# A wavelet convolution block: channel sums by row-wise matmuls, or by two rounded-part matmuls per tile with the means routed through DRAM

## The chip, the cores and the metric

One core of a Trainium2 chip runs the whole kernel. The metric is the device time of one execution in microseconds (us). The engines are TensorE (PE), VectorE (DVE), ScalarE (ACT), GpSimd (POOL) and SyncE (SP), whose queue issues most DMAs.

## The reference, cut to what matters

The input x is 8 images of 256 channels, 160x160 pixels. `haar_dwt` turns it into four bands of 80x80 pixels; a 1x1 convolution with batch norm and ReLU gives `fused` (256 channels). What the change touches is the spatial attention:

```python
avg_sp = jnp.mean(fused, axis=1, keepdims=True)
max_sp = jnp.max(fused, axis=1, keepdims=True)
sp_in = jnp.concatenate([avg_sp, max_sp], axis=1)
sp_map = conv7x7(sp_in)                       # one 80x80 map per image
spatial_out = jax.nn.sigmoid(sp_map) * fused  # the gate
```

Then come channel attention (mean and maximum of each channel of `spatial_out`, a small MLP, sigmoid), a 1x1 projection to 1024 channels with batch norm and ReLU, the inverse transform, and the addition of x.

## The kernel before, in words

**Tiles.** Each image is cut into 14 tiles of 6 or 5 rows of its 80x80 map (`ROWS`: 6, 6, 6, 6, 6, 5, 5, twice), so a tile has 480 or 400 pixels. Channels lie on the 128 partitions, in two halves. There are 112 tiles in all.

**Slots.** The program of every engine is a list of 133 slots. In slot k the first stage works on tile k (`fusion`, L497) and the last stage on tile k-21 (`project`, L483): the two run 21 tiles apart, since the attention of an image needs all of it. Slots 0 to 20 have a first stage only, slots 21 to 111 have both, slots 112 to 132 a last stage only. The engines meet by semaphores, and each works through its list strictly in order.

**First stage.** SP loads x. ACT rounds it to a high part (`x_hi`, L576), DVE takes the rest (`x_lo`, L746). PE multiplies in three products (high by high, high by low, low by high), 24 matmuls of 480 or 400 columns for each half of the input, so `fusion` is 48 matmuls. ACT writes the ReLU to `fused` (L658). `x_hi` of the next tile's first half can be written once `fusion` of this tile's first half is done, and its second half once the whole is.

**Last stage.** ACT and DVE split the gated tile into `y_hi` (L628) and `y_lo` (L824). PE projects, 48 matmuls, ACT and DVE form sums and differences (L606, L781, L783), DVE writes the pixels (`cells`, L801), and x is added, by an accumulating DMA from POOL's queue (L411), or in the last 21 tiles by DVE and POOL (L281). SP stores.

**Attention of image b-1**, in the first eight slots of image b (called phases 0 to 7):
- Channel sums: POOL adds the two halves of tile k-1 to `sm` (`channel_sum`, L404), after `x_lo` of the next tile's first half. PE sums over the partitions at the end of the slot (`add_channels`, L516): for each row one matmul of 80 columns, whose weight block `pick` has a single column of ones, so that the sum falls into that row's partition of `sums`. The operands are plain float32, and each such matmul shows as two records in the trace: 12 or 10 a slot.
- Channel maxima: DVE (L840, L849, L852), in phase 0 to DRAM and back into `maps[:, 1]` (SP, L351 and L362).
- Phase 1: ACT copies the means from `sums` into `maps[:, 0]` (L649), PE convolves after both halves of `fusion` (`convolve`, L525), ACT takes the sigmoid (L622), SP stores it to DRAM (L334).
- Phases 2 to 5: SP loads the sigmoid broadcast in chunks of 800 pixels (`sigb`, L328, the next one once the last was used), DVE gates two chunks a slot (`gate`, L817), ACT sums them in the next slot (`chunk_means`, L615).
- Phase 6: DVE reduces the partial results (`pool`, L886), PE starts the MLP (L563) at the slot's end. Phase 7: PE's `project` waits for the new channel weights and the first `y_lo`.

The orders of DVE, ACT, PE and SP within a slot stand in the four `body` functions. In the tail `cell` is a buffer of its own, and the last image's gate is loaded into the space of `xin` and `x_hi`.

Of the kernel before, what the change touches and what calls it, by code (L numbers as in the profile page):

```python
# [12 lines left out]
P = 128  # L13
# [31 lines left out]
def haar_block(nc, x, fusion_w, fusion_b, bn1_g, bn1_b, bn1_m, bn1_v, sa_w, ca_w1, ca_w2,  # L45
# [26 lines left out]
    map_dram = nc.dram_tensor("map_scratch", [1, NPX], F32, kind="Internal").ap()  # L72
    sig_dram = nc.dram_tensor("sig_scratch", [1, NPX], F32, kind="Internal").ap()
# [18 lines left out]
    with ExitStack() as ctx:  # L92
# [3 lines left out]
        def sem(name):  # L96
# [15 lines left out]
        cell = sb("cell", [P, XPM])  # L112
        sm = sb("sm", [P, PXM])
        sigb = sb("sigb", [P, CPX])
# [4 lines left out]
        pick = sb("pick", [P, 2 * GROUP - 1])  # L119
# [18 lines left out]

        mx = sd[:, 0, 0:PXM]
# [7 lines left out]


        last_gate = [xin[:, :, :].rearrange("p a b -> p (a b)")[:, 0:NPX // 2],
                     x_hi[:, :, :].rearrange("p a b -> p (a b)").bitcast(F32)[:, 0:NPX // 2]]  # L150
# [6 lines left out]
        tmp = cell[:, 0:4 * C].rearrange("p (q c) -> p q c", q=4)  # L157
# [8 lines left out]
        sums = pm[0:H2, 0:W2]  # L166
# [12 lines left out]
        ones_ready = sem("ones_ready")  # L179
        var_ready = sem("var_ready")  # L180
# [27 lines left out]
        sm_ready = sem("sm_ready")  # L208
        sum_psum = sem("sum_psum")
        across_psum = sem("across_psum")  # L210
        mean_ready = sem("mean_ready")
        maxima_ready = sem("maxima_ready")
# [28 lines left out]

        LL, LH, HL, HH = range(4)
# [43 lines left out]
        def _(sp):  # L286
# [43 lines left out]

            def store_sig(s):
                need(sp, mult_done, CT * NCH * s.nb)
                sp.wait_ge(sig_ready, s.nb + 1)
                sp.dma_start(sig_dram.rearrange("o (h w) -> (o h) w", w=W2), sig[:, :]).then_inc(sig_stored, 16)  # L334

            def body(s):
                if s.phase in GATED and s.a:
                    load_sig(s, GATED[s.phase][0])
# [44 lines left out]
        def _(gp):  # L383
# [3 lines left out]
            nc.gpsimd.memset(pick[:, :], 0.0).then_inc(pool_mem, 1)  # L387
            gp.wait_ge(pool_mem, 3)
            nc.gpsimd.memset(pick[:, GROUP - 1:GROUP], 1.0).then_inc(ones_ready, 1)
# [6 lines left out]
            def channel_sum(s):  # L396

                k = s.k - 1
                n = px_of(k)
                gp.wait_ge(f_ready, CT * (k + 1))  # L400
                if s.load_next:
                    gp.wait_ge(xlo_ready[0], s.k + 2)
                need(gp, sum_psum, k)
                nc.gpsimd.tensor_tensor(sm[:, 0:n], fused[:, 0, ring(k)], fused[:, 1, ring(k)],  # L404
                                        ALU.add).then_inc(sm_ready, 1)
# [34 lines left out]
        def _(pe):  # L440
# [29 lines left out]
            pe.wait_ge(ones_ready, 2)  # L470
# [35 lines left out]
            def add_channels(s):  # L506

                k = s.k - 1
                pe.wait_ge(sm_ready, k + 1)
                if s.phase == 1:  # L510
                    pe.wait_ge(mean_ready, s.nb + 1)
                for r in range(ROWS[k % TILES]):
                    row = FIRST[k % TILES] + r
                    at, base = row % GROUP, row - row % GROUP
                    m = min(GROUP, H2 - base)
                    mm = pe.matmul(sums[base:base + m, :], pick[:, GROUP - 1 - at:GROUP - 1 - at + m],  # L516
                                   sm[:, r * W2:(r + 1) * W2], start=(at == 0), stop=(at == m - 1))
                mm.then_inc(sum_psum, 1)

            def convolve(s):  # L520
                pe.wait_ge(mean_ready, s.nb + 1)
                pe.wait_ge(map_landed, 16 * (s.nb + 1))
                pe.wait_ge(band_pass, KS * NK)
                for j in range(NK):
                    mm = pe.matmul(conv, band[:, j, :], maps[:, j // KS, j % KS:j % KS + W2],  # L525
                                   start=(j == 0), stop=(j == NK - 1))
                mm.then_inc(conv_psum, 1)
# [44 lines left out]
        def _(act):  # L572
# [4 lines left out]

            act.wait_ge(var_ready, 2)
# [51 lines left out]

            def body(s):
                if s.phase == LAST:
                    act.wait_ge(hid_psum, s.nb + 1)
                    nc.scalar.activation(hid[:, :], squeezed, ACT.Relu).then_inc(hid_ready, 1)
# [11 lines left out]
                if s.phase == 1:  # L646
                    act.wait_ge(sum_psum, s.k - 1)
                    need(act, conv_psum, s.nb)
                    nc.scalar.activation(maps[:, 0, PAD:PAD + W2], sums, ACT.Copy, scale=1.0 / C  # L649
                                         ).then_inc(mean_ready, 1)  # L650
# [27 lines left out]
        def _(dve):  # L678
# [107 lines left out]
            def cells(s, i):  # L786
# [3 lines left out]
                if adding(s.kc, i):  # L790
                    need(dve, stored[g % 3], 16 * (g // 3))
                    to = xre[:, g % 3, 0:4 * n_px]
                else:
                    need(dve, added_v, plain_upto(g - 1))
                    need(dve, added_p, plain_upto(g - 1))
                    to = cell[:, 0:4 * n_px]
# [66 lines left out]

            def body(s):
# [18 lines left out]
                if s.phase == LAST - 1:  # L883
# [3 lines left out]
                    nc.vector.tensor_reduce(pool[:, :, 1], part[:, 1, :, :], AX.X, ALU.max).then_inc(pool_ready, 1)  # L887
                if s.phase in GATED:
# [56 lines left out]
```

## Time and profile before

| what | value |
|---|---|
| median of 3 runs | 2567.86 us (2566.55 to 2569.47) |
| profiled execution, its own time | 2566.07 us |
| its span, first to last instruction | 2564.3 us |
| PE matmul busy | 2429.5 us, 95% |
| DVE busy | 2066.0 us, 81% |
| ACT busy | 1072.1 us, 42% |
| POOL busy | 388.1 us, 15% |
| granted TensorE clock, mean | 0.987 |

The profiled execution lies 1.8 us below the median, and its span another 1.8 us below its own time. A row of a timeline gives start, length, engine, line, operation, output<-inputs and shape; in brackets stands the idle time of the engine before it and what ended that. "x12" is a merged row of twelve. Matmuls are pipelined, so the distance of their starts counts, not their length.

### The profile page before, as it was taken

Reading aid. Unit: us, or ns where it says so; the run is one execution under the profiler, and the core shown is the slowest. Engines: PE = TensorE matmul, PEld = TensorE weight load, DVE = VectorE, ACT = ScalarE, POOL = GpSimd, SP = SyncE. Lnnn points to the kernel's source line nnn. Section 1 sums busy time; section 2 is a strip of 40 time slices with the busy share of each in tenths; the row PEclk is TensorE's granted clock in tenths of the full one; section 3 lists DMA queues with packets and bytes.
Section 4 is the critical chain, followed back from the end, with each engine's and each line's share of the span. In section 5 each row is a group of like instructions: output and inputs, shape, how many; then the busy total and the mean of one; then the engine's idle time right before and its main releaser. Section 6 shows DMA issues by size and latency. Waiting matters only on the chain. (4 is left out here: it accounts for less than half of the span.)

```text
span 2564.3 us, 32151 instructions
## 1 busy us (share of the span) xinstructions
PE 2429.5 (95%) x12373; PEld 2121.6 (83%) x12373; DVE 2066.0 (81%) x2611; ACT 1072.1 (42%) x1421; POOL 388.1 (15%) x347
## 2 busy tenths in 40 slices
PE   5999999999999999999999999999999999986886
PEld 4888889898898978888898888989888888975765
DVE  4756778797778887788787987788877888779898
ACT  3444534354344533455334543445434453324222
POOL 0010111111111111111111111111111111122233
PEclk9999999999999999999999999999999999988999
DMA  4445699999999999999999999999999999886687
GB/s 142 159 159 178 183 279 273 269 294 262 253 276 272 294 254 258 281 273 285 261 265 271 287 271 271 270 274 292 256 260 268 281 291 258 232 286 243 247 289 281
DMA packets 110301, 660.26 MB, mean 257 GB/s; under 512 B 15362, under 2 KB 16452, under 8 KB 109892
## 3 DMA queue, kind: packets, MB, share of 16 engines
q1 hardware_dynamic: 83940, 487.80, 50.1%
q0 software_dynamic: 26208, 170.41, 36.5%
q8 instruction: 97, 1.59, 0.2%
q14 instruction: 56, 0.46, 0.0%
HBM read 448.04 MB, written 210.12 MB: 257 GB/s over the span
## 5 line engine op out<-in xcount | busy, mean ns | idle before, releaser
L483 PE MATMUL pp<-y_hi,wp_hi 128*128 128x480 f32 (+1 forms) x1792 | 677.4, 378 | 75.5 <-DVE y_lo L824 45.2
L746 DVE TENSOR_TENSOR x_lo<-xin,x_hi 128x1920 fp32r<-128x1920 f32 (+1 forms) x224 | 461.9, 2063 | 318.9 <-ACT x_hi L576 318.8
L576 ACT ACTIVATE x_hi<-xin 128x1920 fp32r<-128x1920 f32 (+1 forms) x224 | 418.1, 1867 | 671.1 <-PE pf L497 671.1
L497 PE MATMUL pf<-x_hi,wf_hi 128*128 128x480 f32 (+1 forms) x1792 | 677.7, 378 | 11.3 <-DVE wp_lo L741 6.2
L483 PE MATMUL pp<-y_lo,wp_hi 128*128 128x480 f32 (+1 forms) x1792 | 671.0, 374 | 0.0
L483 PE MATMUL pp<-y_hi,wp_lo 128*128 128x480 f32 (+1 forms) x1792 | 668.6, 373 | 0.0
L497 PE MATMUL pf<-x_hi,wf_lo 128*128 128x480 f32 (+1 forms) x1792 | 665.3, 371 | 0.0
L497 PE MATMUL pf<-x_lo,wf_hi 128*128 128x480 f32 (+1 forms) x1792 | 664.7, 371 | 0.0
L483 PEld LDWEIGHTS pp<-y_hi,wp_hi 128*128 128x128 f32 x1792 | 341.6, 191 | 133.9 <-DVE y_lo L824 61.1
L606 ACT ACTIVATE relu<-pp,t 128x480 f32<-128x480 f32 (+1 forms) x448 | 285.1, 640 | 397.3 <-PE pp L483 357.2
L801 DVE SCALAR_TENSOR_TENSOR xre<-sd,both 128x960 f32<-128x960 f32 (+1 forms) x364 | 410.3, 1169 | 6.5
L497 PEld LDWEIGHTS pf<-x_hi,wf_hi 128*128 128x128 f32 x1792 | 337.1, 188 | 62.4 <-DVE wp_lo L741 6.5
L483 PEld LDWEIGHTS pp<-y_hi,wp_lo 128*128 128x128 f32 x1792 | 341.4, 191 | 40.0
L483 PEld LDWEIGHTS pp<-y_lo,wp_hi 128*128 128x128 f32 x1792 | 341.2, 190 | 38.9
L411 POOL DMA_DIRECT2D xre<-in_x_dram x182 | 160.2, 880 | 1395.5 <-DVE xre L801 1395.5
L497 PEld LDWEIGHTS pf<-x_lo,wf_hi 128*128 128x128 f32 x1792 | 337.3, 188 | 40.0
L497 PEld LDWEIGHTS pf<-x_hi,wf_lo 128*128 128x128 f32 x1792 | 337.6, 188 | 37.0
L781 DVE SCALAR_TENSOR_TENSOR sd<-pp,nbias,relu 128x480 f32<-128x480 f32 (+1 forms) x448 | 308.1, 688 | 27.1 <-PE pp L483 16.5
L783 DVE SCALAR_TENSOR_TENSOR sd<-pp,nbias,relu 128x480 f32<-128x480 f32 (+1 forms) x448 | 306.4, 684 | 0.0
L658 ACT ACTIVATE fused<-pf,t 128x480 f32<-128x480 f32 (+1 forms) x224 | 138.6, 639 | 293.4 <-PE pf L497 275.0
L404 POOL TENSOR_TENSOR sm<-fused 128x480 f32<-128x480 f32 (+1 forms) x112 | 134.3, 1199 | 563.3 <-issue 293.7
L824 DVE SCALAR_TENSOR_TENSOR y_lo<-fused,ch,y_hi 128x480 fp32r<-128x480 f32 (+1 forms) x224 | 150.8, 715 | 1.0 <-ACT y_hi L628 1.0
(89 smaller groups left out, 1180.7 us busy)
## 6 DMA issues: line engine op xcount, KB each, us to landing
xin<-in_x_dram SPq DMA_DIRECT2D x160, 960.0 KB, 6.7
out_dram<-xre SPq DMA_DIRECT2D x160, 960.0 KB, 5.2
xre<-in_x_dram POOLq DMA_DIRECT2D x130, 960.0 KB, 9.3
xin<-in_x_dram SPq DMA_DIRECT2D x64, 800.0 KB, 6.5
out_dram<-xre SPq DMA_DIRECT2D x64, 800.0 KB, 4.5
xre<-in_x_dram POOLq DMA_DIRECT2D x52, 800.0 KB, 8.9
xre<-in_x_dram SPq DMA_DIRECT2D x30, 960.0 KB, 6.6
sigb<-sig_scratch SPq DMA_DIRECT2D x56, 400.0 KB, 7.9
```

The lines of the kernel that those rows point to most:

```text
L404: nc.gpsimd.tensor_tensor(sm[:, 0:n], fused[:, 0, ring(k)], fused[:, 1, ring(k)], ALU.add).then_inc(sm_ready, 1)
L411: nc.gpsimd.dma_start(xre[:, g % 3, 0:4 * px_of(kc)], dram(x_v, kc, i), accum_op=ALU.add).then_inc(x_added[g % 3], 16)
L483: mm = pe.matmul(pp[j][:, 0:n_px], w[:, kt, cols], y[:, s.pc, kt, 0:n_px], start=(kt == 0 and m == 0), stop=(kt == CT - 1 and m == 2))
L497: mm = pe.matmul(pf[o][:, 0:n_px].rearrange("p (y w) -> p y w", w=W2), w[:, i, q, o * P:(o + 1) * P], v[:, q % 2, :, q // 2, :], start=(i ...
L576: nc.scalar.activation(halves(x_hi, i, k), pairs(i, k), ACT.Copy).then_inc(xhi_ready[i], 1)
L606: nc.scalar.activation(relu[:, n, 0:n_px], pp[j][:, 0:n_px], ACT.Relu, bias=bias2[:, j * CT + i:j * CT + i + 1]).then_inc(r_ready, 1)
L658: nc.scalar.activation(fused[:, o, ring(s.k)], pf[o][:, 0:px_of(s.k)], ACT.Relu, bias=bias1[:, o:o + 1]).then_inc(f_ready, 1)
L746: nc.vector.tensor_tensor(halves(x_lo, i, k), pairs(i, k), halves(x_hi, i, k).bitcast(F32), ALU.subtract).then_inc(xlo_ready[i], 1)
L781: nc.vector.scalar_tensor_tensor(rows[:, :, 0, :], p, low, q, ALU.max, ALU.add).then_inc(sd_ready, 1)
L783: nc.vector.scalar_tensor_tensor(rows[:, :, 1, :], p, low, q, ALU.max, ALU.subtract).then_inc(sd_ready, 1)
L801: nc.vector.scalar_tensor_tensor(px[:, :, :, c], s0, both[:, c, i:i + 1], s1, ALU.add, op).then_inc(cell_ready, 1)
L824: nc.vector.scalar_tensor_tensor(y_lo[:, kc % 2, i, 0:n_px], fused[:, i, ring(kc)], ch[:, i:i + 1], y_hi[:, kc % 2, i, 0:n_px].bitcast(F32 ...
```

## The change

Five edits go together.

1. The sum over partitions is made for a whole tile at once. `sm` is split into `sm_hi` (ACT, rounded to float32r) and `sm_lo` (DVE, the rest), and two matmuls of 480 or 400 columns add the tile's sums into partition t of `sums`, t being the tile's number in the image. `pick` is float32r, with 14 of its columns used as weights.
2. ACT gets `sum_upper`, after `upper` and before `chunk_means` and the ReLUs of `fused`; DVE gets `sum_lower`, after `lower` and before the gate and `channel_max`. `add_channels` waits for `sm_lo`, POOL waits for `sm_lo` instead of the sum before it writes `sm` again.
3. The means now lie as 14 partitions of up to 6 rows, while the convolution wants one row in each of 80 partitions. ACT writes them to `means` (a part of `sigb`) at the head of phase 1; SP stores them to DRAM, waits, and loads them into `maps[:, 0]` with four DMAs (35, 5, 35 and 5 rows). `convolve` waits for these.
4. `cell` takes the space of `xin[:, 0]`, and the last image's gate that of `x_lo` and `x_hi`.
5. `pick` is built in `sm` and copied by ACT at the start.

```diff
+    mean_dram = nc.dram_tensor("mean_scratch", [TILES, PXM], F32, kind="Internal").ap()
-        cell = sb("cell", [P, XPM])
+        sm_hi = sb("sm_hi", [P, PXM], F32R)
+        sm_lo = sb("sm_lo", [P, PXM], F32R)
-        pick = sb("pick", [P, 2 * GROUP - 1])
+        pick = sb("pick", [P, 2 * TILES - 1], F32R)
+        means = sigb[0:TILES, 0:PXM]
+        cell = xin[:, 0, :]
-        sums = pm[0:H2, 0:W2]
+        sums = pm[0:TILES, 0:PXM]
+        ENDS = [t + 1 for t in range(TILES) if ROWS[t] < RMAX]
+        RUNS = list(zip([0] + ENDS[:-1], ENDS))
...
+            def store_means(s):
+                sp.wait_ge(mean_ready, s.nb + 1)
+                sp.dma_start(mean_dram, means).then_inc(mean_stored, 16)
+
+            def load_means(s):
+
+                sp.wait_ge(mean_stored, 16 * (s.nb + 1))
+                for t0, t1 in RUNS:
+                    rows = FIRST[t1 - 1] + ROWS[t1 - 1] - FIRST[t0]
+                    sp.dma_start(maps[FIRST[t0]:FIRST[t0] + rows, 0, PAD:PAD + W2],
+                                 mean_dram.rearrange("t (r w) -> (t r) w", w=W2)[t0 * RMAX:t0 * RMAX + rows, :]
+                                 ).then_inc(mean_landed, 16)
...
             def body(s):
+                if s.phase == 1:
+                    store_means(s)
+                    load_means(s)
                 if s.phase in GATED and s.a:
                     load_sig(s, GATED[s.phase][0])
...
-                need(gp, sum_psum, k)
+                need(gp, smlo_ready, k)
                 nc.gpsimd.tensor_tensor(sm[:, 0:n], fused[:, 0, ring(k)], fused[:, 1, ring(k)],
                                         ALU.add).then_inc(sm_ready, 1)
...
             def add_channels(s):
 
                 k = s.k - 1
-                pe.wait_ge(sm_ready, k + 1)
+                pe.wait_ge(smlo_ready, k + 1)
                 if s.phase == 1:
                     pe.wait_ge(mean_ready, s.nb + 1)
-                for r in range(ROWS[k % TILES]):
-                    row = FIRST[k % TILES] + r
-                    at, base = row % GROUP, row - row % GROUP
-                    m = min(GROUP, H2 - base)
-                    mm = pe.matmul(sums[base:base + m, :], pick[:, GROUP - 1 - at:GROUP - 1 - at + m],
-                                   sm[:, r * W2:(r + 1) * W2], start=(at == 0), stop=(at == m - 1))
+                t, n = k % TILES, px_of(k)
+                for part_of in (sm_hi, sm_lo):
+                    mm = pe.matmul(sums[:, 0:n], pick[:, TILES - 1 - t:2 * TILES - 1 - t], part_of[:, 0:n],
+                                   start=(t == 0 and part_of is sm_hi), stop=(t == TILES - 1 and part_of is sm_lo))
                 mm.then_inc(sum_psum, 1)
 
             def convolve(s):
-                pe.wait_ge(mean_ready, s.nb + 1)
+                pe.wait_ge(mean_landed, 16 * len(RUNS) * (s.nb + 1))
                 pe.wait_ge(map_landed, 16 * (s.nb + 1))
...
+            def mean(s):
+                act.wait_ge(sum_psum, s.k - 1)
+                need(act, mult_done, CT * NCH * s.nb)
+                nc.scalar.activation(means, sums, ACT.Copy, scale=1.0 / C).then_inc(mean_ready, 1)
+
+            def sum_upper(s):
+                n = px_of(s.k - 1)
+                act.wait_ge(sm_ready, s.k)
+                need(act, sum_psum, s.k - 1)
+                nc.scalar.activation(sm_hi[:, 0:n], sm[:, 0:n], ACT.Copy).then_inc(smhi_ready, 1)
+
             def body(s):
+                if s.phase == 1:
+                    mean(s)
...
-                if s.phase == 1:
-                    act.wait_ge(sum_psum, s.k - 1)
-                    need(act, conv_psum, s.nb)
-                    nc.scalar.activation(maps[:, 0, PAD:PAD + W2], sums, ACT.Copy, scale=1.0 / C
-                                         ).then_inc(mean_ready, 1)
+                if s.turn:
+                    sum_upper(s)
                 for c in GATED.get(s.phase - 1, ()) if s.phase else ():
                     chunk_means(s, c)
...
+            def sum_lower(s):
+                n = px_of(s.k - 1)
+                dve.wait_ge(smhi_ready, s.k)
+                need(dve, sum_psum, s.k - 1)
+                nc.vector.tensor_tensor(sm_lo[:, 0:n], sm[:, 0:n], sm_hi[:, 0:n].bitcast(F32),
+                                        ALU.subtract).then_inc(smlo_ready, 1)
...
+                if s.turn:
+                    sum_lower(s)
                 if s.phase in GATED:
                     gate(s, GATED[s.phase][0])
```

## Rows read from the trace of the kernel before

**Rows 1.** The page, its first part: busy us, share of the span, instructions
```profile
PE 2429.5 (95%) x12373; PEld 2121.6 (83%) x12373; DVE 2066.0 (81%) x2611; ACT 1072.1 (42%) x1421; POOL 388.1 (15%) x347
```

**Rows 2.** Timeline of PE, one full slot: one sum block to the next
```profile
1239.40 1.02 PE L516 MATMUL pm<-sm,pick 128*32 128x80 f32 x12
...
1240.67 0.38 PE L497 MATMUL pf<-x_hi,wf_lo 128*128 128x480 f32 x1
...
1261.23 0.38 PE L483 MATMUL pp<-y_lo,wp_hi 128*128 128x480 f32 x1
1261.54 1.02 PE L516 MATMUL pm<-sm,pick 128*32 128x80 f32 x12
```

**Rows 3.** Timelines of PE, ACT, DVE and POOL in the first image, one slot
```profile
155.16 1.02 PE L516 MATMUL pm<-sm,pick 128*32 128x80 f32 x12 [0.38 <-POOL sm L404]
...
161.73 1.94 ACT L576 ACTIVATE x_hi<-xin 128x1920 fp32r<-128x1920 f32 x1 [4.40 <-PE pf L497]
...
163.70 2.16 DVE L746 TENSOR_TENSOR x_lo<-xin,x_hi 128x1920 fp32r<-128x1920 f32 x1 [2.91 <-ACT x_hi L576]
...
165.99 1.21 POOL L404 TENSOR_TENSOR sm<-fused 128x480 f32<-128x480 f32 x1 [10.89 <-DVE x_lo L746]
...
166.26 1.32 ACT L658 ACTIVATE fused<-pf,t 128x480 f32<-128x480 f32 x2 [2.59 <-PE pf L497]
...
167.26 1.02 PE L516 MATMUL pm<-sm,pick 128*32 128x80 f32 x12 [0.38 <-POOL sm L404]
```

**Rows 4.** Waits between 60 and 226 us: total us, times, longest
```profile
PEld pm L516 <- POOL sm L404: 12.2, 14, 1.8
```

**Rows 5.** Groups by line and shape: busy us, mean ns, idle before
```profile
L658 ACT ACTIVATE fused<-pf,t 128x480 f32<-128x480 f32 x160 | 103.2, 660 | 240.2 <-PE pf L497 221.9 <-DVE y_lo L824 18.3
...
L840 DVE TENSOR_TENSOR sd<-fused 128x480 f32<-128x480 f32 x80 | 52.6, 658 | 67.3 <-ACT fused L658 67.1
```

**Rows 6.** Waits of DVE between 489 and 583 us: total us, times, longest
```profile
DVE x_lo L746 <- ACT x_hi L576: 7.8, 5, 4.7
DVE fused L817 <- DMA sigb<-sig_scratch: 2.7, 2, 2.4
```

**Rows 7.** Timelines of PE and DVE, end of the gated slots of that image
```profile
584.82 0.62 PE L516 MATMUL pm<-sm,pick 128*32 128x80 f32 x10
...
585.19 0.17 DVE L886 TENSOR_REDUCE pool<-part 128x2 f32<-128x16 f32 x1 [2.19 <-ACT relu L615]
...
599.92 0.48 PE L483 MATMUL pp<-y_hi,wp_hi 128*128 128x480 f32 x1 [2.67 <-DVE y_lo L824]
```

**Rows 8.** Timelines of SP and PE around the convolutions of images 0, 1 and 7
```profile
221.71 0.33 SPq L362 DMA_DIRECT2D maps<-map_scratch  x1
...
223.68 2.17 PE L525 MATMUL pm<-maps,band 80*80 80x80 f32 x28
...
458.04 0.32 SPq L351 DMA_DIRECT2D map_scratch<-maxima  x1
...
462.68 0.32 SPq L362 DMA_DIRECT2D maps<-map_scratch  x1
...
473.72 2.17 PE L525 MATMUL pm<-maps,band 80*80 80x80 f32 x28
...
2272.37 0.32 SPq L362 DMA_DIRECT2D maps<-map_scratch  x1
...
2277.22 3.99 PE L525 MATMUL pm<-maps,band 80*80 80x80 f32 x28 [4.68 <-issue]
```

**Rows 9.** Tile maps: DMA to landing of its 8 loads
```profile
DMA to landing us min/median/max: 1.6/3.3/8.1
```

**Rows 10.** Tile sig: DMA to landing of its 8 stores
```profile
DMA to landing us min/median/max: 4.5/6.3/8.5
```

**Rows 11.** Stretches: PE, PEld, DVE, ACT, POOL busy us, PEclk, DMA share, GB/s
```profile
595.00:607.00 12.00, 9.33 (x37) 7.63 (x35) 9.38 (x10) 6.44 (x10) 2.25 (x2) 0.86 0.77 224
...
2390.00:2540.00 150.00, 121.45 (x552) 100.40 (x550) 146.32 (x184) 42.50 (x69) 50.51 (x23) 1.00 0.82 291
```

More of the change, by code:

```diff
@@ L145, in haar_block @@
         junk = relu[:, :, :].rearrange("p a b -> p (a b)").bitcast(BF16)[:, 0:CPX]
-        last_gate = [xin[:, :, :].rearrange("p a b -> p (a b)")[:, 0:NPX // 2],
-                     x_hi[:, :, :].rearrange("p a b -> p (a b)").bitcast(F32)[:, 0:NPX // 2]]
+        cell = xin[:, 0, :]
+        last_gate = [v[:, :, :].rearrange("p a b -> p (a b)").bitcast(F32)[:, 0:NPX // 2] for v in (x_lo, x_hi)]
         stage = fused[:, 1, 2 * THIRD * W2:3 * THIRD * W2]
@@ L156, in haar_block @@
         pw = stage2[:, 0:NB * C].rearrange("p (t c) -> p t c", t=NB)
-        tmp = cell[:, 0:4 * C].rearrange("p (q c) -> p q c", q=4)
+        tmp = sd[:, :, :].rearrange("p a b -> p (a b)")[:, 0:4 * C].rearrange("p (q c) -> p q c", q=4)
         tmp2 = stage2[:, 8 * C:12 * C].rearrange("p (q c) -> p q c", q=4)
@@ L179, in haar_block @@
         ones_ready = sem("ones_ready")
+        pick_ready = sem("pick_ready")
         var_ready = sem("var_ready")
@@ L208, in haar_block @@
         sm_ready = sem("sm_ready")
+        smhi_ready = sem("smhi_ready")
+        smlo_ready = sem("smlo_ready")
         sum_psum = sem("sum_psum")
@@ L211, in haar_block @@
         mean_ready = sem("mean_ready")
+        mean_stored = sem("mean_stored")
+        mean_landed = sem("mean_landed")
         maxima_ready = sem("maxima_ready")
@@ L386, in _ @@
             nc.gpsimd.memset(maps[:, :, :], 0.0).then_inc(ones_ready, 1)
-            nc.gpsimd.memset(pick[:, :], 0.0).then_inc(pool_mem, 1)
+            nc.gpsimd.memset(sm[:, 0:2 * TILES - 1], 0.0).then_inc(pool_mem, 1)
             gp.wait_ge(pool_mem, 3)
-            nc.gpsimd.memset(pick[:, GROUP - 1:GROUP], 1.0).then_inc(ones_ready, 1)
+            nc.gpsimd.memset(sm[:, TILES - 1:TILES], 1.0).then_inc(ones_ready, 1)
             nc.gpsimd.affine_select(out=ident[:, :], in_=ident[:, :], compare_op=ALU.not_equal, fill=1.0,
@@ L469, in _ @@
             pe.wait_ge(wflo_ready, 4)
-            pe.wait_ge(ones_ready, 2)
+            pe.wait_ge(pick_ready, 1)
             def project(s, i):
@@ L576, in x_upper @@
                 nc.scalar.activation(halves(x_hi, i, k), pairs(i, k), ACT.Copy).then_inc(xhi_ready[i], 1)
+            act.wait_ge(ones_ready, 2)
+            nc.scalar.activation(pick[:, :], sm[:, 0:2 * TILES - 1], ACT.Copy).then_inc(pick_ready, 1)
             act.wait_ge(var_ready, 2)
@@ L795, in cells @@
                     need(dve, added_p, plain_upto(g - 1))
+                    dve.wait_ge(xlo_ready[CT - 1], NT)
                     to = cell[:, 0:4 * n_px]
```

## The prediction

> **What bounds the kernel now.** I read the page first: PE is busy 95% of the span, DVE 81%, ACT 42%, POOL 15% [rows 1]. An average over stages says little about one edit, so I cut the trace at PE's sum blocks, which close every slot. In slots 21 to 111, both stages at work, PE sets the pace. The reader should see in [rows 2] that a six-row slot takes 22.14 us from block to block, and that the 94 steps from the second `fusion` matmul (1240.67) to the last `project` matmul (1261.23) take 20.56 us, 0.219 us each. The 96 matmuls cost 21.0 us; the twelve small ones cost the other 1.14 us. Where PE alone is late, that is what the change can shorten.
>
> Three stretches obey something else. In the first image a slot takes 12.10 us (155.16 to 167.26) with 48 matmuls, 10.5 us: PE waits for POOL's `sm` in 14 slots [rows 3, 4]. There the sum block closes a loop: block, `fusion` of the first half, `x_hi` at 161.73, `x_lo` at 163.70, `sm` at 165.99 to 167.20, next block at 167.26. In the gated slots (phases 2 to 6) DVE is almost full: between 489 and 583 us it waits 7.8 us for `x_hi`, of which 4.7 ahead of the first gate, and 2.7 us for the gate's chunks, so some 6 us in four slots [rows 6]. In the last 21 slots DVE is busy 146.32 of 150 us [rows 11].
>
> **1. The sum block on PE.** Twelve small matmuls go, two of 480 columns come. None of 14 weight columns is in the trace; the nearest rows are those of 480 columns, 0.219 us a step, and these stream the same columns of the same type: 0.44 us. The other end: the old block needs 1.14 us for 12 x 80 = 960 columns, as many as two times 480; at its pace per column nothing is gained. I take 0.44. A six-row tile saves 0.70 us, a five-row tile (ten small matmuls, 0.95 us, against 0.36) about 0.6; 14 tiles save 9.6 us. I take 0.68 a block where PE is the bound.
>
> **2. `sum_upper` and `sum_lower`.** The nearest rows: ACT writes 480 columns in 0.66 us (L658), DVE combines two SBUF tiles of 480 in 0.66 (L840) [rows 5], some 0.6 when it streams behind another. In ordinary full slots ACT is idle when `sm` ends, and DVE waits for `fused` before `channel_max` (67.1 us over 80 tiles, 0.84 each, more than the 0.6 added) [rows 5]: cost nothing there.
>
> In the first image both lie on the loop. Behind `sm` now come 0.66 + 0.66 us and a second handoff, together 1.4 us, before the block starts; the block is 0.70 shorter. ACT also does `sum_upper` ahead of `fused` (which stood at 166.26), so `fused` comes about 1.7 us later, still in time for the shorter block's end. Slot: 12.10 + 1.4 - 0.70 = 12.8 us. For 19 slots, five-row ones a little less: **+13.5 us**. Slots 21 to 27 save 7 x 0.68: **-5 us**.
>
> **3. Full images with gated slots.** There are six such rounds of 14 slots (slots 28 to 111). Nine blocks of each are PE-bound: 9 x 0.68 = 6.1 us, one of them ahead of the first gate. In the other five slots (phases 2 to 6) DVE gets 0.6 us more each and PE asks for all 0.7 us sooner. I followed DVE from the first gate to `pool` at 585.19. Four `sum_lower` lie on the way, 2.4 us. Of the 6 us idle about 3.4 can be used up: the chunk wait shrinks only by the 0.6 of the one `sum_lower` between issue and use, and in two slots DVE still waits 0.5 us for ACT, which sums its chunks before it writes `fused`. So the chain gains 3.4 - 2.4 = 1.0 us where PE's blocks would give 3.4, and PE waits at the slot's end for `sum_lower` and `pool` (before: block at 584.82, `pool` at 585.19, met within 0.4 us [rows 7]). Phase 7 hangs on the same DVE chain (PE waits 2.67 us for `y_lo` at 599.92 [rows 7]) and moves with it. A round: 6.1 + 1.0 = 7.1 us; six: **-43 us**. Bounds: DVE gives back all (9.6 a round, -58), or the five slots gain nothing (-37).
>
> **4. The means through DRAM.** Before, ACT wrote them 5 us ahead of the convolution. Now: ACT writes 14 partitions of 480 at the head of phase 1 (0.66 us by L658; only `x_hi`, which waits for PE, is queued behind it), SP issues the store behind the load of the maxima (L362), waits S, issues four loads of some 0.3 us each, and the last lands after L. The route is 0.3 + S + 1.1 + L from L362's issue. L: 1.6/3.3/8.1 us [rows 9]. S: a small store took 4.5/6.3/8.5 [rows 10]; the maxima's took at most 4.6 (458.04 to 462.68) [rows 8]. I take 5.5. While SP waits, the load of tile k+2, the stores and residual loads stand behind it for some 5 us; the x load is for the tile after the next, most of a slot (22.14 us) ahead of its use, so nothing more is late.
>
> - Image 1 (images 2 to 6 alike): L362 at 462.68, convolution at 473.72, 11.0 us, 10.3 with the earlier block. Route 10.2: just in time. By the spread of L, two of the six meet a slow queue: about 4.5 us each, 9 us.
> - Image 0 has no last stage: 221.71 to 223.68 is 2.0 us. Route with a fast queue 0.3 + 4.5 + 1.1 + 1.6 = 7.5: 5.5 us late.
> - Image 7: 2272.37 to 2277.22 is 4.85 us, and the convolution waited for its map already. Route 10.8: 6 us late, and `project` of the next slot, the last gate's load and DVE behind them move along.
> - After a wait of 2.67 us for `y_lo` the granted clock averaged 0.86 over 12 us [rows 11]: part of it went at the lower level, 1.2 of 2.4 GHz, 1.7 us lost. I add it for two of the long waits, 3 us.
>
> Together **+23 us**. Lower bound: all hidden but images 0 and 7, +8. Upper: every image with the slowest store and load, 18 us against 10.3, 7.7 late each, about +60.
>
> A rule speaks for the lower bound: the Trainium skill, "DMA: Bandwidth & Descriptors", section "Anatomy of one DMA", gives a fixed cost of about 2.0 us for a DMA from GpSimd's queue. With S and L of 2 us, an estimate from that page, the route is 5.4 us, and only images 0 (3.4) and 7 (0.6) are late, +4 us. The trace's small transfers, behind 960 KB ones, took 3.3 and 6.3 in the median, so the sum goes by them.
>
> **5. The rest.** `cell`, the last gate's place and `pick` add one 14-to-27-column copy at the start: nothing. In the tail one block less of 0.7 us is hidden by DVE.
>
> **Sum.** 13.5 - 5 - 43 + 23 = -11.5 us. On the profiled execution 2566.07 becomes 2554.5 (span 2564.3 to 2552.8); on the median, 1.8 us above it, 2567.86 becomes **2556 us**.
>
> **The rivals.** What a measurement here can tell from no change is about 0.2%, 5.1 us.
>
> (a) *The route is hidden* in images 1 to 6: for it, half of the maxima's loads land within 3.3 us; against it, the slowest took 8.1. Part 4 is then +8, or +4 by the page's rule: 2537 to 2541. Chance 0.22.
>
> (b) *The convolution waits for the means in every image*: SP's store, wait and four loads take the place of ACT's copy. For it: the store lies on the queue behind a 960 KB store and beside POOL's accumulating load; against it: 10.3 us of slack. Price 7.7 + 1.7 us at the upper end for each of seven images and 6 to 10 for image 7, some +65: 2598 at most. It decides the sign from part 4 = 35 us, 4.4 us an image. With 6 us each, +50: 2583. Chance 0.14.
>
> (c) *TensorE's clock falls in the first image*, because PE now idles about 1.9 us of each 12.8. Price 1.7 us in up to 19 slots: +32, 2588. Against it: in the tail PE idled 19% of 150 us and the clock read 1.00 [rows 11]. Chance 0.04.
>
> (d) *The change doesn't do what it says*: float32r with 14 weight columns runs at the old pace. Then parts 1 and 3 vanish and `sum_lower` stays: 13.5 x 2 + 23 = +50 at the worst, 2618. Chance 0.04.
>
> My forecast itself, 2545 to 2565: chance 0.56.
>
> **How the numbers follow.** The range reaches down to (a) with a full gain in part 3 and up to the middle of (b): 2532 to 2580. Faster than 2562.7: all of (a) and four fifths of the forecast, 0.66. Within 0.2%: the forecast's edge and a little of (b), 0.16. Slower: (b), (c), (d), 0.18.
>
> **What would show it.** Right: the full slot measures about 21.4 us instead of 22.14; the first image's slot 12.8 instead of 12.10, with PE waiting for `sm_lo`; PE's block at the end of phase 6 waits for DVE; the waits list has the convolution waiting on DMA, long in images 0 and 7. Wrong: a two-matmul block of over 0.6 us, a PE clock under 1 in the first image, or a convolution that waits over 4 us in every image.

## The result, and the profile after

The changed kernel takes 2581.96 us (median of 6 runs, 2578.03 to 2586.69) beside 2568.66 us of the kernel before in the same comparison: ratio 1.0051, 95% interval 1.0036 to 1.0066. It is 0.5% slower where 0.5% faster was forecast, and lies just above the range. The profiled execution took 2583.17 us, its span grew from 2564.3 to 2581.4, by 17.1 us.

The page of the changed kernel, its first two parts (they answer to [rows 1]):

```profile
span 2581.4 us, 30569 instructions
...
PE 2386.6 (92%) x11317; PEld 2080.6 (81%) x11317; DVE 2127.0 (82%) x2723; ACT 1133.1 (44%) x1535; POOL 387.8 (15%) x347
...
PE   5888789999999999999999989999999999976886
...
PEclk9998899999999999999999999999999999988998
DMA  4444469999999989999999999999899999986687
```

PE has 43 us less to do and the kernel is longer all the same. The digits point at slices 2 to 6, the first image: PE reads 8, 8, 8, 7, 8 there, where every slice read 9 before, and its clock falls to 8 in slices 4 and 5.

The full slot, in PE's timeline of the changed kernel (it answers to [rows 2]), is as forecast:

```profile
1266.82 0.38 PE L545 MATMUL pm<-sm_hi,pick 128*14 128x480 f32 x1
1267.03 0.38 PE L545 MATMUL pm<-sm_lo,pick 128*14 128x480 f32 x1
...
1288.25 0.38 PE L545 MATMUL pm<-sm_hi,pick 128*14 128x480 f32 x1
```

21.43 us from block to block instead of 22.14. So part 1 holds: 0.7 us a block (a five-row slot falls from 18.65 to 17.96 us). Cutting both traces at the sum blocks, as the prediction did, gives the account in us (span after less span before):

| stretch | forecast | measured |
|---|---|---|
| start to slot 20, image 0's convolution (slot 15) left out | +13.5 | +42.8 |
| slot 15 | +5.5 | +4.0 |
| slots 21 to 27 | -5 | -3.0 |
| six rounds, slots 28 to 111 | -43, +9 for the means | -30.3 |
| slot 112 and the tail | +6 | +3.6 |
| clock after long waits | +3 | in the rows above |
| sum | -11 | +17.1 |

The prediction rounded part 4 down by half a microsecond, and so wrote -11.5. Of the 42.8 us in the first row, 1.5 come before the first block, 18.2 in slots 2 to 14 and 23.1 in slots 16 to 20.

**The first image.** The timeline of the changed kernel there (it answers to [rows 3]; in between, two slots):

```profile
151.46 0.38 PE L528 MATMUL pf<-x_lo,wf_hi 128*128 128x480 f32 x1
154.28 0.58 PE L545 MATMUL pm<-sm_hi,pick 128*14 128x480 f32 x1 [2.45 <-DVE sm_lo L910]
154.66 0.60 PE L545 MATMUL pm<-sm_lo,pick 128*14 128x480 f32 x1
155.06 0.60 PE L528 MATMUL pf<-x_hi,wf_hi 128*128 128x480 f32 x1
155.46 0.60 PE L528 MATMUL pf<-x_hi,wf_lo 128*128 128x480 f32 x1
...
168.49 0.39 PE L545 MATMUL pm<-sm_hi,pick 128*14 128x480 f32 x1 [1.70 <-DVE sm_lo L910]
...
178.70 1.21 POOL L435 TENSOR_TENSOR sm<-fused 128x480 f32<-128x480 f32 x1 [11.60 <-DVE x_lo L787]
179.94 0.60 ACT L671 ACTIVATE sm_hi<-sm 128x480 fp32r<-128x480 f32 x1 [3.57 <-POOL sm L435]
...
180.58 0.66 DVE L910 TENSOR_TENSOR sm_lo<-sm,sm_hi 128x480 fp32r<-128x480 f32 x1 [2.01 <-ACT sm_hi L671]
181.29 0.39 PE L545 MATMUL pm<-sm_hi,pick 128*14 128x480 f32 x1 [1.70 <-DVE sm_lo L910]
```

This slot, 168.49 to 181.29, follows no fall of the clock and takes 12.80 us, the forecast to the digit. But at 154.28, after 2.45 us of idling, PE goes on with matmuls 0.40 us apart instead of 0.22: the lower of the two clock levels, 1.2 GHz. The stretches of slots 2 to 14 (after and before; columns as in [rows 11]) show the sum of it: the clock averages 0.95 where it was 1.00.

```profile
62.30:232.00 169.70, 145.01 (x653) 123.99 (x654) 105.32 (x176) 68.41 (x66) 14.98 (x13) 0.95 0.43 143
```

```profile
60.80:212.30 151.50, 144.87 (x777) 125.62 (x777) 98.25 (x163) 63.36 (x53) 15.05 (x13) 1.00 0.48 161
```

**Slots 16 to 20** grew most, from 58.3 to 81.4 us. From the timelines of POOL, ACT and PE of the changed kernel, end of slot 18:

```profile
291.23 1.22 POOL L435 TENSOR_TENSOR sm<-fused 128x480 f32<-128x480 f32 x1 [15.86 <-DVE x_lo L787]
292.48 0.60 ACT L671 ACTIVATE sm_hi<-sm 128x480 fp32r<-128x480 f32 x1 [3.24 <-POOL sm L435]
292.99 0.85 ACT L646 ACTIVATE relu<-fused 128x800 bf16<-128x800 f32 x1
...
296.01 0.87 ACT L646 ACTIVATE relu<-fused 128x800 bf16<-128x800 f32 x1
...
296.88 1.19 ACT L699 ACTIVATE fused<-pf,t 128x480 f32<-128x480 f32 x2
297.67 0.67 PE L528 MATMUL pf<-x_hi,wf_hi 128*128 128x400 f32 x1 [3.23 <-ACT fused L699]
```

ACT works strictly in order, and `sum_upper` stands ahead of `chunk_means`. So ACT stood idle for 3.24 us until POOL's `sm`, then summed four chunks, and only then wrote `fused`, for which PE waited 3.23 us before the `fusion` of slot 19 (at 297.67). In the kernel before, the chunk sums came first and ended about when `sm` was ready, and `fused` followed at once:

```profile
260.41 1.22 POOL L404 TENSOR_TENSOR sm<-fused 128x480 f32<-128x480 f32 x1 [10.47 <-DVE x_lo L746]
...
262.01 0.19 ACT L615 ACTIVATION_READ_ACCUMULATOR relu<-fused 128x1 f32 x1
262.10 1.20 ACT L658 ACTIVATE fused<-pf,t 128x480 f32<-128x480 f32 x2
```

**The convolution** (it answers to [rows 8]). Waits over the whole span of the changed kernel (total us, times, longest), then its SP and PE around the convolution of image 7:

```profile
PE pm L545 <- DVE sm_lo L910: 52.9, 25, 6.3
...
PE pm L554 <- DMA maps<-mean_scratch: 15.1, 4, 8.4
DVE fused L859 <- DMA sigb<-sig_scratch: 14.3, 19, 1.5
```

```profile
2285.61 0.43 SPq L348 DMA_DIRECT2D mean_scratch<-sigb  x1
2291.97 1.29 SPq L355 DMA_DIRECT2D maps<-mean_scratch  x4
...
2294.38 4.03 PE L554 MATMUL pm<-maps,band 80*80 80x80 f32 x28 [8.43 <-DMA maps<-mean_scratch]
```

PE waited for the means in images 0, 2, 5 and 7: 2.89, 0.75, 3.00 and 8.43 us (the last against 4.68 before). The store of the means, from its issue to the issue of the loads, took 1.60 us in image 0, where no last stage moves data, 6.36 us here, and 7.23 us at most (image 5).

**The gated slots.** Slots 30 to 33 keep 0.7 us each in the six full images. Slot 34 (phase 6) gives it back: 21.35 us in the mean where it was 18.65. Its end on DVE and PE, second of the six images:

```profile
922.48 0.17 DVE L935 TENSOR_REDUCE pool<-part 128x2 f32<-128x16 f32 x1 [2.18 <-ACT relu L646]
...
922.64 0.57 DVE L910 TENSOR_TENSOR sm_lo<-sm,sm_hi 128x400 fp32r<-128x400 f32 x1
923.26 0.35 PE L545 MATMUL pm<-sm_hi,pick 128*14 128x400 f32 x1 [2.48 <-DVE sm_lo L910]
```

PE waits there for `sm_lo`, which stands behind `pool` in DVE's list, 2.3 us in the mean; in the kernel before, its block waited for nobody in these slots. This is the wait that the prediction named for the end of phase 6.

### The profile page after: what moved, and what is told of

It is laid out like the page before. It is cut to its first block and busy times, and to the rows that moved or that the text cites. A ratio compares the mean times of both kernels' runs of the same rounds, so it can differ in the third digit from the quotient of the medians.

```text
span 2581.4 us, 30569 instructions
## 1 busy us (share of the span) xinstructions
PE 2386.6 (92%) x11317; PEld 2080.6 (81%) x11317; DVE 2127.0 (82%) x2723; ACT 1133.1 (44%) x1535; POOL 387.8 (15%) x347
## 5 line engine op out<-in xcount | busy, mean ns | idle before, releaser
L528 PE MATMUL pf<-x_hi,wf_lo 128*128 128x480 f32 (+1 forms) x1792 | 672.3, 375 | 0.0
L528 PE MATMUL pf<-x_lo,wf_hi 128*128 128x480 f32 (+1 forms) x1792 | 671.5, 375 | 0.0
L528 PEld LDWEIGHTS pf<-x_hi,wf_hi 128*128 128x128 f32 x1792 | 342.8, 191 | 75.1 <-issue 19.4
L528 PEld LDWEIGHTS pf<-x_hi,wf_lo 128*128 128x128 f32 x1792 | 342.8, 191 | 40.4
```

Source lines behind the costliest of these rows:

```text
L528: mm = pe.matmul(pf[o][:, 0:n_px].rearrange("p (y w) -> p y w", w=W2), w[:, i, q, o * P:(o + 1) * P], v[:, q % 2, :, q // 2, :], start=(i ...
```

## The experiments

All but three edit the changed kernel; the ratio is to the kernel before, run on the same chip. Theory A at the start: ACT's order and the loop in the first image (with the clock that it lets fall), the route of the means, and something in the gated slots each take their part. Each was tested alone. The medians are of the execution times, while stretches are cut from the one profiled execution of each kernel.

### ACT's order

```diff
-                if s.turn:
+                if s.turn and s.c:
                     sum_upper(s)
                 for c in GATED.get(s.phase - 1, ()) if s.phase else ():
                     chunk_means(s, c)
+                if s.turn and not s.c:
+                    sum_upper(s)
```

> Edit: in the slots without a last stage (1 to 20), ACT sums the gated chunks (chunk_means) before it rounds sm (sum_upper), instead of after. Output as before. Theory A (the rounding, waiting for POOL's sm, holds back four chunk sums and with them fused and the next fusion): slots 17 to 20, 67.0 us together in the changed kernel against 46.2 before, fall to about 52; the gaps of 3.6 us between the two-matmul block and fusion vanish, and the whole becomes 12 to 16 us shorter, about 2567. Rival B (these slots are long because DVE waits for sm_hi ahead of its gate, whatever ACT's order): they stay within 3 us of 67.

2564.47 us (10 runs, 2558.21 to 2591.06), ratio 0.9989 (0.9962 to 1.0016). The same five slots in this kernel and in the changed one, by stretches:

```profile
249.20:313.10 63.90, 53.37 (x253) 46.09 (x253) 43.70 (x62) 38.91 (x57) 5.87 (x5) 0.98 0.59 188
```

```profile
249.50:330.90 81.40, 59.02 (x253) 50.38 (x253) 44.08 (x62) 39.43 (x57) 5.86 (x5) 0.88 0.47 154
```

17.5 of the 23.1 us are gone, and the clock is back from 0.88 to 0.98: the order of two calls on ACT cost about as much as all that slots 2 to 14 lost (18.2 us). The medians say 0.6%, some 16 us. The profiled execution is only 10.1 us shorter than the changed kernel's, since its six rounds took 8.4 us longer, for a reason that wasn't looked for.

### No route

The convolution waits for ACT's means in place of the loads; store and loads are gone, so the map of means that it reads stays zero.

```diff
-                if s.phase == 1:
-                    store_means(s)
-                    load_means(s)
...
-                pe.wait_ge(mean_landed, 16 * len(RUNS) * (s.nb + 1))
+                pe.wait_ge(mean_ready, s.nb + 1)
```

> Edit: the store and the four loads of the means are left out, the convolution waits for ACT's means only, and reads zeros in place of the means (left out: the mean's part of the map). Theory A (the route costs only where the convolution waits for its landing: about 4 us in image 0, 1 in image 2, 5 in image 5, 4 in image 7): 12 to 16 us shorter than the changed kernel. Rival B (SP held up by its wait delays loads and stores elsewhere, and costs more than the visible waits): over 25 us shorter. Rival C (the visible waits are covered by other waits): under 5 us shorter.

2569.66 us (2565.79 to 2577.36), ratio 0.9992 (0.9980 to 1.0004): 0.6% under the changed kernel's 1.0051, or some 12 to 15 us; by the profiled executions 6 us (this one was among its slower ones). Slot 15 took 13.0 us instead of 17.5. The route costs something like 12 us, half of the 23 that the prediction gave it.

### Filling PE's gap in the first image

Six matmuls of 480 columns, whose results nobody reads, stand ahead of each block, so that PE hardly idles.

```diff
+                if not s.c:
+                    for j in range(FILL):
+                        pe.matmul(pp[j % 4][:, 0:480], wp_hi[:, 0, 0:P], wp_hi[:, 0, 0:480], start=True, stop=True)
```

> Edit: in slots 1 to 20 PE does six more matmuls of 480 columns (products of the projection weights into a psum tile that nothing reads) ahead of its wait for sm_lo, 1.3 us of work in a gap of 2.1. Output as before. Theory A (in slots 1 to 14 five falls of the granted clock, 1.7 us each, come from PE's gaps): those slots, 232.0 us to the block of slot 14, end at about 223.5, the clock reads 1.00 up to there, and the whole is 8 us or more shorter. Rival B (the slots are long by the handoffs alone): no shorter, or longer by the added matmuls.

2581.04 us, ratio 1.0032 (1.0017 to 1.0047). Its stretch of slots 2 to 14:

```profile
62.60:226.50 163.90, 154.28 (x731) 132.47 (x732) 105.17 (x176) 68.31 (x66) 15.15 (x13) 1.00 0.45 148
```

The clock stays at 1.00 and slots 2 to 14 lose 6 us (169.7 to 163.9): slots 4, 7, 9, 13 and 14 are 0.6 to 1.6 us shorter each, the others as they were. So the clock costs 6 us there, less than expected, and the loop the other 12.4, 0.95 us a slot instead of 0.70. Without the falls slots 2 and 9 to 14 grew by 0.6 to 0.8 us, as forecast, but slots 3 to 8 by 1.0 to 1.4. In these DVE also builds the band matrices (84 operations of 0.29 us between 80.7 and 149.2); that this is why was not tried.

### A sixteenth of `sum_lower`

DVE subtracts 16 columns only in phases 2 to 6 of the full images; the low part of the other sums is stale.

```diff
             def sum_lower(s):
                 n = px_of(s.k - 1)
...
+                if s.c and s.phase in (2, 3, 4, 5, 6):
+                    n = 16
```

> Edit: in phases 2 to 6 of the slots with both stages, sum_lower works on 16 columns instead of 480 or 400 (left out: the low part of those tiles' channel sums, stale values take its place). Theory A (in the gated slots DVE is the bound, and 5 sum_lower of 0.6 us a round lie on its chain): each of the six rounds gets 2 to 3 us shorter, 12 to 18 us together, and PE's wait at the end of phase 6 shrinks. Rival B (ACT's chain of chunk sums sets phase 6, and sum_lower on DVE is covered): under 4 us together.

2584.21 us (2574.22 to 2598.75), ratio 1.0048 (1.0027 to 1.0069): no faster than the changed kernel. In the profiled executions the six gated stretches (slot 29's block to slot 34's in each full image) add up to 618.9 us instead of 622.0, 0.5 us a round, less than they differ between kernels that are alike there (620 to 630). So with these transfers in the way, DVE's 2.4 us of `sum_lower` are not what eats the gated slots' gain. The edit was not tried where the transfers are thin.

### POOL's sum early in the first image

In the slots without a last stage POOL no longer waits for `x_lo` of the next tile before it writes `sm`. The second kernel does the same to the kernel before.

```diff
-                if s.load_next:
+                if s.load_next and s.c:
                     gp.wait_ge(xlo_ready[0], s.k + 2)
```

> Edit: in slots 1 to 20 POOL adds the two halves of the last tile as soon as they are there, without waiting for x_lo of the next tile. Output as before. Theory A (a loop fusion, x_hi, x_lo, sm, sm_hi, sm_lo, sum block sets slots 1 to 14, and PE's gap in it makes the clock fall): the loop is cut, slots 2 to 14, 169.7 us in the changed kernel and 151.5 before, fall under 150, the clock reads 1.00 there, chunk sums no longer stand behind sm, and the whole gets 30 to 45 us shorter, about 2545. Rival B (the slots are set by PE, ACT or x loads beside the loop): under 10 us shorter. Rival C (POOL and DVE get in each other's way): x_lo on DVE takes longer than 2.16 us and eats half of it.

> Edit to the kernel BEFORE: the same early sm (no wait of POOL for x_lo in slots 1 to 20). Output as before. Theory A (the same loop set the first image's slots before, at 12.10 us instead of 10.5 + 1.1): slots 2 to 14 fall from 151.5 to about 145, the whole by 6 to 12 us. It tells how much of the gain of the early sm belongs to the change and how much was there to be had before. Rival B: no difference, since before the change PE waited for sm by 0.4 us only.

Changed kernel: 2539.29 us (4 runs, 2524.67 to 2553.00), ratio 0.9878 (0.9834 to 0.9922). Kernel before: 2560.20 us, ratio 0.9962 (0.9947 to 0.9976). Slots 2 to 14 of the first, by stretch:

```profile
60.60:200.70 140.10, 136.57 (x653) 117.67 (x652) 104.48 (x176) 70.12 (x66) 20.96 (x13) 1.00 0.52 174
```

and its waits there:

```profile
PE pm L545 <- DVE sm_lo L910: 3.5, 6, 1.5
```

140.1 us instead of 169.7, and less than the 151.5 of the kernel before. The loop is broken, the clock stays up. With the same edit in both, the change is 0.8% faster: the loss in the first image had turned its sign.

### Two buffers for the gate's chunks, alone and with the early sum

```diff
-        sigb = sb("sigb", [P, CPX])
+        sigb = sb("sigb", [P, 2, CPX])
...
-                need(sp, mult_done, CT * (NCH * s.nb + c))
-                sp.dma_start(sigb[:, :], sig_dram[:, c * CPX:(c + 1) * CPX].to_broadcast([P, CPX])
+                need(sp, mult_done, CT * (NCH * s.nb + max(c - 1, 0)))
+                sp.dma_start(sigb[:, c % 2, :], sig_dram[:, c * CPX:(c + 1) * CPX].to_broadcast([P, CPX])
```

> Edit: two buffers for the gate's chunks instead of one, so that the load of a chunk no longer waits for the last one's use. Output as before. Shrinking sum_lower in the gated slots gave only some 0.6 us a round. Theory A (the serial chain of chunk load of 8 us and gate of 2 us sets the gated slots): DVE's waits for the chunks, 14.3 us in all, vanish, PE's wait at the end of phase 6 shrinks, and each of six rounds gets 1 to 3 us shorter, 8 to 18 together. Rival B (DVE's own work fills these slots, and the chunk waits only take up what is free anyway): under 4 us together.

> Edit: both of the two above, the early sm and the two chunk buffers. Output as before. If both parts hold, their gains add: 35 to 55 us below the changed kernel, 2525 to 2545, faster than the kernel before by 1% or more. If the gated slots are DVE's own (rival B of the chunk buffers), it is within 4 us of the early sm alone.

2609.39 us (4 runs, 2582.84 to 2618.80), ratio 1.0135 (1.0078 to 1.0191): clearly slower. With the early sum 2536.30 us, ratio 0.9872 (0.9845 to 0.9899), the same as without the buffers. Waits over the whole span of the first:

```profile
PE pm L554 <- DMA maps<-mean_scratch: 30.5, 5, 7.2
DVE fused L859 <- DMA sigb<-sig_scratch: 22.7, 23, 2.2
```

Chunks asked for earlier took longer to land (median 9.3 us after issue, against 8.3), and the convolution's waits doubled (15.1 to 30.5 us): of the 35 us that the six rounds lost in the profiled execution, 26 lie in the convolution's slots. The buffer isn't what is short. That pointed at the transfers themselves: the changed kernel's stretch of gated slots in a full image has the DMA engines at 0.99 (next to the last column; 0.98 in the kernel before, 1083 to 1191).

```profile
1112.00:1220.00 108.00, 105.09 (x511) 93.04 (x509) 97.18 (x132) 56.04 (x85) 14.71 (x15) 1.00 0.99 291
```

### Thin chunks, in both kernels

```diff
+                rows = P if s.nb == 0 else 16
-                sp.dma_start(sigb[:, :], sig_dram[:, c * CPX:(c + 1) * CPX].to_broadcast([P, CPX])
+                sp.dma_start(sigb[0:rows, :], sig_dram[:, c * CPX:(c + 1) * CPX].to_broadcast([rows, CPX])
```

> Changed kernel with the spatial gate's chunk loads brought to 16 partitions instead of 128 in every image after the first (most of the gate's values are then stale, that part of the product is left out; the multiply runs over the same elements). Theory A, transfers set the pace of the gated slots (the DMA engines are 98% busy there): the six stretches from slot 29's sum block to slot 34's, 102 to 104.5 us in the changed kernel, fall by 2 to 4 us each, the convolution's waits for the means shrink as the small transfers find shorter queues, and the kernel ends 15 to 30 us earlier. Rival B, the engines' chains set it: the six stretches stay within 1 us of the changed kernel's, the end moves by less than 5 us.

> The kernel before with the same thinner chunk loads. It gives what the change itself is worth in a full round where transfers aren't in the way: theory A says that this kernel, too, gets faster by 10 us or more, and that the changed one with thin chunks gains about 7 us in a round over this one, as the prediction had it (the convolution's waits left out). Rival B: this kernel stays within 5 us of the kernel before, and the changed one gains 5 to 6 us a round over it, as with full chunks.

Changed kernel: 2576.85 us (10 runs, 2565.40 to 2582.00), ratio 1.0012 (0.9997 to 1.0027); the profiled execution, at 2566.73, was one of the fastest. Kernel before: 2561.89 us, ratio 0.9967 (0.9954 to 0.9980). In the profiled one the gated stretches agreed with theory A (101.8 to 102.2 us each), but the gains in the medians, 0.4% or 10 us of the changed kernel and 8.5 us of the kernel before, lay between theory A and rival B. The first image and the convolutions of the changed kernel spread its executions over 17 us, so the question was put again where both are quiet (below).

### The store of the means in phase 0, and the best version

```diff
             def body(s):
                 if s.phase == 1:
-                    store_means(s)
                     load_means(s)
...
                 if s.phase == 0:
+                    store_means(s)
                     sp.wait_ge(maxima_ready, s.nb + 1)
```

> Changed kernel with SP's store of the means issued in phase 0, ahead of the wait for the maxima, instead of at the head of phase 1; the loads stay where they are. If the route itself costs time (prediction, part 4), the store's trip is hidden behind the maxima's: the convolution's waits for the means fall from 15 us over four images to under 5, image 7's from 8.4 to about 4.7, and the kernel ends 8 to 12 us earlier. Rival: the store, now behind a full queue and ahead of SP's other work, is no quicker, and the end moves by less than 4 us.

> Changed kernel with both: POOL's wait for the next tile's low part dropped from its channel sum in the first image, and the store of the means in phase 0. If the two costs are separate, the gains add: 42 us of the first and 8 to 12 us of the second, 2525 to 2535 us, 1.0 to 1.5% below the kernel before. Rival: transfers that now come sooner wait elsewhere and give the second part back: 2537 to 2545 us.

Early store alone: 2571.47 us (10 runs), ratio 1.0007 (0.9997 to 1.0016), 0.4% or 11 us under the changed kernel; span 12.1 us shorter. Its SP and PE around image 7's convolution:

```profile
2267.57 1.98 SPq L348 DMA_DIRECT2D mean_scratch<-sigb  x1
...
2275.92 1.30 SPq L355 DMA_DIRECT2D maps<-mean_scratch  x4
...
2280.46 3.99 PE L554 MATMUL pm<-maps,band 80*80 80x80 f32 x28 [4.96 <-issue]
```

Image 7 waits 4.96 us, near the 4.68 before the change; image 0 still 1.22 us, images 1 to 6 not at all. That agrees with the run without the route: as built, the route costs 11 to 12 us, and nearly all of it can be hidden by placing one call elsewhere.

Both edits together: **2521.06 us** (4 runs, 2520.46 to 2523.70), ratio 0.9807 (0.9792 to 0.9822), 1.9% below the kernel before, 2.4% below the changed one, under the 2525 to 2535 expected. Waits over its whole span:

```profile
PE pm L545 <- DVE sm_lo L910: 20.6, 15, 2.8
DVE fused L859 <- DMA sigb<-sig_scratch: 17.6, 21, 1.7
...
PE pm L554 <- DMA maps<-mean_scratch: 1.4, 1, 1.4
```

### Thin chunks in the quiet kernels

The same edit of the chunk loads, now in the best version and in the kernel before with the early sum.

> The fastest kernel so far (POOL's sum early in the first image, the store of the means in phase 0) with the gate's chunk loads on 16 partitions after the first image (most of the gate's values stale, that part of the product left out). Its first image and its convolutions hardly wait, so what is left of the full rounds is seen alone. Theory A, transfers hold the gated slots back once PE is quicker: its six rounds, slots 27 to 111, take 1765 to 1769 us (294.5 each) instead of 1777.5, every gated stretch 101.8 to 102.2 us instead of 102.3 to 105.6, and the median lies 8 to 12 us under 2521. Rival B, the thin run's even rounds were one lucky execution: 1774 us or more and a median within 4 us of 2521.

> The kernel before with POOL's sum early in the first image (no other part of the change) and the same thin chunk loads: the control of the run above. Theory A: the kernel before keeps its PE pace whatever the chunks do, its rounds go from 1816.2 us to 1808 to 1811 us, less than the changed kernel's, and the difference between the two thin kernels over the six rounds is 40 to 44 us, the 7.1 a round of the prediction. Rival B: both gain alike and the difference stays at 36 to 39 us, as with full chunks.

2509.18 us (5 runs, 2508.92 to 2513.66), ratio 0.9765 (0.9751 to 0.9778); and 2553.01 us (2549.52 to 2554.76), ratio 0.9926 (0.9914 to 0.9939). The six rounds as one stretch each (slot 27's block to slot 111's; kernel before, changed kernel, best, best thin, kernel before with early sum and thin chunks, in this order):

```profile
434.90:2249.20 1814.30, 1796.21 (x9254) 1578.36 (x9254) 1485.28 (x1815) 791.07 (x1054) 248.46 (x252) 1.00 0.94 270
```

```profile
478.60:2262.60 1784.00, 1748.15 (x8462) 1535.60 (x8460) 1530.80 (x1899) 837.23 (x1138) 248.04 (x252) 1.00 0.96 276
```

```profile
423.20:2200.70 1777.50, 1747.75 (x8462) 1536.37 (x8461) 1530.60 (x1899) 837.37 (x1138) 248.12 (x252) 1.00 0.96 277
```

```profile
423.50:2190.00 1766.50, 1740.65 (x8461) 1533.36 (x8460) 1528.95 (x1899) 837.07 (x1138) 248.00 (x252) 1.00 0.95 269
```

```profile
427.90:2237.90 1810.00, 1794.54 (x9254) 1576.94 (x9253) 1485.57 (x1815) 790.73 (x1054) 247.92 (x252) 1.00 0.93 262
```

The second number is the length. With thin chunks the change is worth 1810.0 - 1766.5 = 43.5 us in six rounds, beside the 43 of the prediction. The six gated stretches (slot 29's block to slot 34's) add up, by the starts of the blocks, to 622.4 us in the kernel before, thin or not, to 621.9 in the changed kernel, 622.2 in the best, but 611.2 in the best with thin chunks. So with full chunks the gated slots keep nothing of PE's gain. With 16 partitions of them they keep 11.2 of the 21 us that five shorter blocks a round would give, about half. DVE's waits for chunks fall from 17.6 to 3.7 us over the whole span:

```profile
DVE fused L860 <- DMA sigb<-sig_scratch: 3.7, 3, 1.4
```

What is left is again in slot 34: 19.6 us (21.3 in the best version with full chunks, 18.0 where PE alone is the bound), its block waiting 1.5 us in the mean for `sm_lo` behind `pool`. Its end in the best version with thin chunks, same image:

```profile
863.99 0.17 DVE L936 TENSOR_REDUCE pool<-part 128x2 f32<-128x16 f32 x1 [2.19 <-ACT relu L647]
...
864.77 0.35 PE L546 MATMUL pm<-sm_hi,pick 128*14 128x400 f32 x1 [1.67 <-DVE sm_lo L911]
```

So two limits lie behind each other: late chunks first (theory A), then the chain of gates, chunk sums and `pool` over DVE and ACT. In the kernel before, PE was slow enough to hide the transfers in the gated slots; thin chunks shortened only slot 35 there, by 1.0 us a round. Whether the second limit is `sum_lower`'s own time, ACT's chunk sums, or the place of `sum_lower` behind `pool` was not tried. The MLP on PE, right behind the block, needs `pool` too, so the place alone can hardly be worth more than `sum_lower`'s 0.6 us, an estimate from these rows.

## Why the prediction was wrong, point by point

- **Part 1** was right: 0.70 us a six-row block. A five-row block gave 0.69 instead of 0.6, so 14 tiles save 9.8 us; the prediction's 9.6 is 9.4 by its own terms.
- **Part 2** failed, and with it the sign: the first image cost 29.3 us more than its +13.5, and all the rest of the account, -25.7 us, lies near the -24.5 forecast. Its 0.7 us a slot was right in slots 2 and 9 to 14 once the falls of the clock are taken out. Three things were missed. The step "ACT also does `sum_upper` ahead of `fused` [...] still in time" looked at the plain slots only; in slots 17 to 20 `chunk_means` stand between the two, and the order cost 17.5 us. The loop was costed from one slot; slots 3 to 8 grew more, and the mean was 0.95 us, some 3 us in all, for a cause that stays open. And rival (c), given 0.04, came true in part: the clock fell in five of slots 2 to 14, 6 us, and more often in slots 16 to 20 (inside the 17.5). A clock under 1 in the first image was one of the prediction's own signs of being wrong. Its argument against, a tail with 19% idle at clock 1.00 [rows 11], compared shares; no single gap in that tail was over 1.84 us, while the five falls came with gaps of 1.92 to 2.81 us.
- **Part 3** named the wait rightly (the block at the end of phase 6, for DVE) and missed what sets it first: the transfers. The prediction read the DMA engines' share only in [rows 11], at 0.77 and 0.82; in the gated slots it is 0.98. With full chunks these slots gained 0.1 us a round instead of 1.0, with thin ones 1.9. That the thin kernels differ by 43.5 us, the forecast's 43, is partly luck: the gated slots gave 11.2 us instead of 6, the other nine blocks of a round 32.3 in all instead of 37, as slot 35 gained nothing (26.0 in both). Whether "DVE gets 0.6 us more each" is the reason for what the thin kernel still loses stays open. With full chunks the best version gains 38.7 us in the rounds over the kernel before with the early sum (1816.2 less 1777.5). The changed kernel's rounds took 6.5 us more than the best version's, 1784.0 against 1777.5; 3.75 of them are the convolution's waits in images 2 and 5. Part 4 had given these rounds +9.
- **Part 4** was oversized: 11 to 12 us, not 23. Image 0 waited 2.9 us instead of 5.5, since its route took 4.5 us and not 7.5 (the store 1.6 instead of 4.5). Image 7 waited 3.8 us longer instead of 6, and two of the six others waited, as forecast, but 0.75 and 3.00 us. The Trainium skill, "DMA: Bandwidth & Descriptors", section "Anatomy of one DMA", gives a fixed cost of about 2.0 us for a DMA from GpSimd's queue. The store here goes from SP's queue: image 0's, 1.60 us, is near that figure; image 7's, 6.36 us behind large transfers, is three times that. Neither number fitted all images.
- **Part 5** held: the tail grew only by what image 7's convolution waited.
- Rivals (a), (b) and (d) didn't happen. Two bounds don't follow from their terms: (b) at its upper end adds up to 72 to 76 us, not 65, and (a) with a full gain in part 3 reaches 2526 us, not 2532.

## What to carry to other kernels

Before an operation is set into an engine's ordered list, look at every variant of the slot for what stands between it and the next result that somebody waits for. When an engine that sets the pace gets faster, read the DMA share of each stage first: what its slowness hid may be the next bound, and here the gated slots kept none of their gain. A total that comes out as forecast proves little until its parts do: 43.5 us against 43 hid two errors of 4 to 5 us each. A handoff added to a loop costs the slots too that had some slack, and where it makes single idle gaps of TensorE longer it can cost clock as well.

## What the runs showed of the hardware that was not expected

The granted clock fell after single gaps of about 2 us. In slots 1 to 14 of the changed kernel PE waited for its block each time. After waits of 1.92, 2.24, 2.29, 2.45 and 2.81 us it ran some eight to ten steps at 0.40 us (0.33 in a tile of five rows), the lower level; after waits of up to 1.75 us it did not. But the longest wait, 3.07 us (block at 114.75), was followed by none, so the length of one gap alone doesn't decide. Filled gaps kept the clock at 1.00. And asking for transfers earlier can make things slower: with two chunk buffers the same bytes took longer to land, and the convolution waited twice as long for its small transfers, 0.8% in all (1.0135 against 1.0051). Beside the early sum the same two buffers made no difference (0.9872 against 0.9878).
